# A cross-attention loop on one core: row 1, the query scales, the last row's low halves, the value products and the output products change places

## The reference

```python
x = x + xattn(layernorm(x), ctx)     # 256 tokens of 512, 4096 keys of 128
x = x + attn(layernorm(x))           # self-attention, 16 heads
x = x + ffn(layernorm(x))            # quantised, 1408 wide

def xattn(hidden_q, kv_c):
    q_hk  = (hidden_q @ Wq.T).reshape(B, S, 16, 128)
    q_big = rope(einsum('bshk,hkq->bshq', q_hk, w_kc_q))        # 384 wide
    kv_r  = rope(kv_c)
    q_r   = einsum('bshq,hqr->bhsr', q_big, W_qr)               # 64 wide
    k_r   = einsum('bld,hdr->bhlr', kv_r, W_kr)
    attn  = softmax(einsum('bhsr,bhlr->bhsl', q_r, k_r))
    ctx_c = einsum('bhsl,bld->bhsd', attn, kv_r)
    ctx   = einsum('bhsd,hkd->bhsk', ctx_c, w_kc_kv)            # the value product
    return merge_heads(ctx) @ Wo.T                              # the output product
```

## Time and profile before

| | us |
|---|---|
| median of the runs (3) | 564.32 |
| lowest and highest | 563.91, 564.53 |
| the profiled execution, its span | 564.2 |

### The profile page before, as it was taken

The page is one execution under the profiler, slowest core; times in us unless marked ns, Lnnn a source line. Parts: engine busy times, 40 slices in busy tenths (PEclk is TensorE's granted clock), DMA queues, the critical chain, the costliest instruction groups (busy, mean ns, idle before and its releaser), DMA issues.

```text
span 564.2 us, 10021 instructions
## 1 busy us (share of the span) xinstructions
PE 528.2 (94%) x3799; PEld 353.0 (63%) x3803; DVE 468.4 (83%) x708; ACT 366.0 (65%) x447; POOL 159.0 (28%) x202
## 2 busy tenths in 40 slices
PE   7899976799999999999999999999997998999996
PEld 3767643366666666666667666766676784455443
DVE  3566997999989999999999999999996447478686
ACT  2125433888788688688688787787786444886441
POOL 2378965101202202202202202202000001496501
PEclk9989999999999999999999999999998998999999
DMA  8979468399999999999999999999999997500001
GB/s 314 345 259 288 156 116 220 87 200 196 198 195 200 202 197 203 208 209 212 203 204 195 203 204 194 198 210 195 204 198 178 226 416 305 238 1 1 1 0 38
DMA packets 287806, 107.41 MB, mean 190 GB/s; under 512 B 276896, under 2 KB 277920, under 8 KB 286368
## 3 DMA queue, kind: packets, MB, share of 16 engines
q1 hardware_dynamic: 287776, 107.01, 87.6%
HBM read 37.26 MB, written 0.52 MB: 67 GB/s over the span
## 4 chain that ended last, share of the span: by engine, by line
PE 57%; DVE 17%; POOL 8%; DMA 6%; issue 6%; ACT 4%; SPq 0%; ACTq 0%; DVEq 0%; POOLq 0%
PE ps L665 15%; PE ps L667 8%; PE ps L647 7%; PE ps L649 7%; PE ps L648 7%; DMA pT<-split 6%; POOL qrope L498 5%; DVE rows L1273 4%; DVE split L1255 3%; PE ps L767 3%; POOL keys L509 2%; POOL stage L510 1%; PE ps L876 1%; PE ps L615 1%; PE ps L617 1%
## 5 line engine op out<-in xcount | busy, mean ns | idle before, releaser
L665 PE MATMUL ps<-pT,VH 128*128 128x256 f16 x1024 | 196.6, 274 | 2.1 <-DMA pT<-split 2.0
L667 PE MATMUL ps<-pT,VL 128*128 128x128 f16 x1024 | 183.3, 220 | 0.0
L1273 DVE TENSOR_SCALAR_CACHE_REDUCE rows<-ps,qback 128x1024 f32<-128x1024 f32 x128 | 163.5, 1280 | 16.0 <-PE ps L649 15.9
L1033 ACT ACTIVATE split<-rows,rz 128x2048 f16<-128x2048 f32 x64 | 124.7, 1994 | 67.8 <-DVE rz L1221 67.7
L1255 DVE SCALAR_TENSOR_TENSOR split<-rows,rz,split 128x2048 f16<-128x2048 f32 x64 | 150.3, 2350 | 1.3 <-issue 1.2
L1019 ACT ACTIVATE rows<-rows,negm 128x2048 f32<-128x2048 f32 x64 | 127.2, 1987 | 0.2 <-DVE negm L1278 0.2
L665 PEld LDWEIGHTS ps<-pT,VH 128*128 128x128 f16 x1024 | 100.5, 98 | 42.6 <-DMA pT<-split 4.8
L667 PEld LDWEIGHTS ps<-pT,VL 128*128 128x128 f16 x1024 | 100.6, 98 | 27.5
L528 POOL TENSOR_TENSOR ctx_c<-acc 128x128 f32<-128x128 f32 x32 | 24.7, 772 | 296.8 <-ACT acc L1008 296.8
L647 PE MATMUL ps<-KH,qcur 128*128 128x512 f16 x256 | 97.1, 379 | 3.3 <-DVE rows L1273 3.3
L649 PE MATMUL ps<-KH,qcur 128*128 128x512 f16 x256 | 97.0, 379 | 0.0
(11 more groups left out here) (175 smaller groups left out, 638.3 us busy)
## 6 DMA issues: line engine op xcount, KB each, us to landing
w_sb<-w SPq DMA_DIRECT2D x3, 2816.0 KB, 15.6
wq_sb<-wq SPq DMA_DIRECT2D x4, 1024.0 KB, 7.3
wo_sb<-wo SPq DMA_DIRECT2D x16, 256.0 KB, 4.2
wkcq_sb<-wkcq SPq DMA_DIRECT2D x4, 768.0 KB, 10.3
keys<-ctxT SPq DMA_DIRECT2D x8, 256.0 KB, 7.1
stage<-ctxT SPq DMA_DIRECT2D x16, 128.0 KB, 9.0
stage<-kcos SPq DMA_DIRECT2D x8, 256.0 KB, 9.0
stage<-ksin SPq DMA_DIRECT2D x8, 256.0 KB, 9.5
```

The costliest lines, as they stand in the source:

```text
L665: nc.tensor.matmul(bank(6 + r % 2, 0, 256), VH[:, 4 * b + k, :], p.rearrange("p x q -> p (x q)"), start=(b == 0 and k == 0), stop=False)
L667: last = nc.tensor.matmul(bank(6 + r % 2, 0, 128), VL[:, 4 * b + k, :], p[:, 0, :], start=False, stop=(b == 7 and k == 3))
L1033: nc.scalar.activation(split[:, split_slot(r, half), :, 0, :], rows[:, k, half * 2048:(half + 1) * 2048].rearrange("p (b k) -> p b k", k=1 ...
L1273: nc.vector.tensor_scalar(rows[:, k, c * 1024:(c + 1) * 1024], ps[:, score_bank(s) * 512:(score_bank(s) + 2) * 512], qback[:, r // 2:r // ...
```

## The change

- **Row 1 ahead of the last heads' queries.** TensorE issues steps 0 to 9 (row 0 and two of row 1) at `p` 18, two more at 19, four at 20, so that both rows stand before the loop. ScalarE takes row 0's two exponentials at `p` 20 ahead of the last two heads' copies, and loads the exponential's table at `p` 17 with a one-column operation.
- **The second query scale inside turn 1**: `query_part` at VectorE's step 5, `query_total` at TensorE's step 10, `query_factor` at VectorE's step 11. The wait for it moves from row 0's to row 1's first values.
- **Loads of `wo` heads 8 to 15**: one behind the transposes of each of rows 4 to 11, instead of all behind the last row.
- **Last turn**: the low halves of row 31 at VectorE's steps 4 and 5 (before: 8 and 10); value products 0 to 3 together at step 8, the others at 16, 17, 18, in banks 0, 1, 4, 5 in turn, with a wait for the fourth product before; their copies at 6 to 9 and 17 to 19; the splits of `wo` at 11 to 16, 20 and 21.
- **Output products by tile**: tile 0 to its end, then tile 1; the last value product behind head 8 of tile 0.

Cut to what is spoken of (functions of ScalarE that only move up in the file are left out):

```diff
-    SPLIT_STEPS = (12, 14, 16, 17, 18, 19, 20, 21)
+    SPLIT_STEPS = (11, 12, 13, 14, 15, 16, 20, 21)
     PRODUCT_STEPS = (18, 19, 20, 21, 22, 23)
+    VALUE_STEPS = (8, 8, 8, 8, 16, 17, 18)
+    CONTEXT_STEPS = (6, 7, 8, 9, 17, 18, 19)
+    VALUE_BANK = (0, 1, 4, 5)
...
             for r in range(2 * XH):
                 turn_row(r)
-            for h in range(XH // 2, XH):
-                sp.dma_start(wo_part(wo_sb, h), wo[:, h, :]).then_inc(wo_in[h // 4], 16)
+                if 4 <= r < 4 + XH // 2:
+                    h = XH // 2 + r - 4
+                    sp.dma_start(wo_part(wo_sb, h), wo[:, h, :]).then_inc(wo_in[h // 4], 16)
...
-                wait(pe, ctxl_lo_done, n - 1)
+                wait(pe, ctxl_lo_done, n - 3)
                 for a in range(2):
-                    last = nc.tensor.matmul(bank(n % 2, a * TOK, (a + 1) * TOK), wkv_sb[:, 2 * n + a, :],
+                    last = nc.tensor.matmul(bank(VALUE_BANK[n % 4], a * TOK, (a + 1) * TOK), wkv_sb[:, 2 * n + a, :],
...
+                if isinstance(i, int) and i == 1 and s == 10:
+                    query_total(1)
+                if last_turn(i) and s == VALUE_STEPS[0]:
+                    for n in range(VALUE_STEPS.count(s)):
+                        value_product(n)
...
+                        pe.wait_ge(qf_done, XH)
+                    if isinstance(i, int) and row == 1 and b == 0:
                         pe.wait_ge(qfac_done, 2)
-                        pe.wait_ge(qf_done, XH)
...
-                if last_turn(i) and s % 2 == 0 and 2 <= s < XH:
-                    value_product(s // 2 - 1)
+                if last_turn(i) and s > VALUE_STEPS[0] and s in VALUE_STEPS:
+                    value_product(VALUE_STEPS.index(s))
...
-                    first = TURN - 16 + (0, 4, 6, 8)[p - 18]
-                    for s in range(first, TURN - 16 + (4, 6, 8, 8)[p - 18]):
+                    first = TURN - 16 + (0, 10, 12, 16)[p - 18]
+                    for s in range(first, TURN - 16 + (10, 12, 16, 16)[p - 18]):
                         attention_step(0, s)
-            query_total(1)
-
-            attention_loop(pe, attention_step, EARLY, AVLAG)
-            for first in (0, XH // 2):
-                for t in range(TT):
-                    for h in range(len(PRODUCT_STEPS) if t == 0 and first == 0 else first, first + XH // 2):
-                        output_product(t, h)
-                        if first == 0 and t == 1 and h == 1:
-                            value_product(XH // 2 - 1)
+
+            attention_loop(pe, attention_step, 2 * EARLY, AVLAG)
+            for t in range(TT):
+                for h in range(len(PRODUCT_STEPS) if t == 0 else 0, XH):
+                    output_product(t, h)
+                    if t == 0 and h == len(PRODUCT_STEPS) + 2:
+                        value_product(XH // 2 - 1)
...
+                if last_turn(i) and s in CONTEXT_STEPS:
+                    context_high(CONTEXT_STEPS.index(s))
+                if last_turn(i) and s in SPLIT_STEPS:
+                    output_weight_high(SPLIT_STEPS.index(s))
...
+                if p == 17:
+                    nc.scalar.activation(warm[:, 1:2], ones[:, 0:1], ACT.Exp).then_inc(warm_done, 1)
...
+                if p == 20:
+                    attention_step(0, TURN - 8)
+                    attention_step(0, TURN - 7)
...
-            attention_loop(act, attention_step, 0, AVLAG)
+            attention_loop(act, attention_step, NCH + 2, AVLAG)
...
+                    if not isinstance(i, int) or row < 2 * XH - 1:
+                        row_low(row, r, s % 8 // 2)
+                if last_turn(i) and s in (4, 5):
+                    row_low(2 * XH - 1, 5, s - 4)
+                if isinstance(i, int) and i == 1 and s == 5:
+                    query_part(1)
+                if isinstance(i, int) and i == 1 and s == 11:
+                    query_factor(1)
...
-                    context_low(s // 2 - 1)
+                if last_turn(i) and s in CONTEXT_STEPS:
+                    context_low(CONTEXT_STEPS.index(s))
...
-            query_part(1)
-            query_factor(1)
```

More of the change, by code:

```diff
@@ L959, in raw_sum @@
                 nc.scalar.activation(absolute[:, :], keys[:, key], ACT.Abs, accum_out=kpart[:, n:n + 1]).then_inc(kabs_done, 1)
[L961 to L967, removed]
[L968 to L989 removed]
             def context_high(n):
                 act.wait_ge(ctxl_ps, n + 1)
[L994 removed]
+                nc.scalar.activation(ctxl_hi[:, 2 * n:2 * n + 2, :].rearrange("p h t -> p (h t)"), bank(VALUE_BANK[n % 4]), ACT.Copy)\
                     .then_inc(ctxl_hi_done, 1)
@@ new lines, in _ @@
+            for p in range(STEPS):
+                if p == 17:
+                    nc.scalar.activation(warm[:, 1:2], ones[:, 0:1], ACT.Exp).then_inc(warm_done, 1)
+                if p % 2 == 0 and p < XH:
+                    act.wait_ge(qhk_done, p // 2 + 1)
+                    nc.scalar.activation(qhk[:, p:p + 2, :].rearrange("p h t -> p (h t)"), bank(0), ACT.Copy)\
+                        .then_inc(qhk_copied, 1)
+                n = p - 6
+                if p == 20:
+                    attention_step(0, TURN - 8)
+                    attention_step(0, TURN - 7)
+                if n >= 0 and n % 2 == 0 and n < XH:
+                    act.wait_ge(qabs_done, n // 2 + 1)
+                    for a in range(2):
+                        nc.scalar.activation(QF[:, n + a, :], absorbed(a), ACT.Copy).then_inc(qf_done, 1)
+                        wait(act, qpart_done, n + a)
+                        nc.scalar.activation(qabsolute[:, :], absorbed(a), ACT.Abs, accum_out=qpart[:, n + a:n + a + 1])\
+                            .then_inc(qpart_done, 1)
+                n = p - 5
+                if n >= 0 and n % 2 == 0 and n < XH:
+                    act.wait_ge(qr_done, n + 2)
+                    wait(act, qabs_done, n // 2 - 1)
+                    nc.scalar.activation(qrT[:, n // 2 % 2, :], bank(6, 0, TOK), ACT.Copy).then_inc(qr_copied, 1)
+                for n in range(1, NCH):
+                    if RAW_STEP[n] == p:
+                        raw_sum(n)
+                for n in range(NCH):
+                    if HIGH_STEP[n] == p:
+                        key_high(n)
+                if p == 15:
+                    act.wait_ge(qhk_done, XH // 2)
+                    act.wait_ge(qfac_done, 1)
+                    nc.scalar.activation(qcur[:, 2, 0], QF[:, 0, :], ACT.Identity, scale=qfac[:, 0:1]).then_inc(qcur_first, 1)
@@ L1233, in key_scale, with row_low @@
                 dve.wait_ge(kscale_done, 2)
+            def row_low(row, r, half):
+                k = r % 3
+                dve.wait_ge(hi_done, 2 * row + half + 1)
+                nc.vector.scalar_tensor_tensor(out=split[:, split_slot(r, half), :, 1, :],
+                                               in0=rows[:, k, half * 2048:(half + 1) * 2048].rearrange("p (b k) -> p b k", k=128),
+                                               scalar=rz[:, k:k + 1], in1=split[:, split_slot(r, half), :, 0, :],
+                                               op0=ALU.mult, op1=ALU.subtract).then_inc(lo_done, 1)
             def query_part(k):
```

35 lines of the change are left out of this document (2 added, 33 removed).

## The result

The changed kernel takes **566.86 us** (median of 19 runs, 563.91 to 569.2), the kernel before 564.32 beside it (19 runs, 560.98 to 566.95). The ratio is 1.0037, with a 95% interval of 1.002 to 1.0055: **slower by 2.1 us** by that ratio, 2.5 by the medians. Forecast were 561.9 and, as a range, 558.6 to 565.2.

What follows compares the result with a forecast made beforehand. TensorE was taken as the bound, with the transpose queue without margin until about 223 us. Loads net of ramp 1.4, last rows -2.2, tiles -0.4, clock -1.75, returned 0.6 gave -2.35: 561.9, range 558.6 to 565.2.

Steps and rivals of the forecast that it cites:

- What bounds the kernel: TensorE is busiest; before about 223 us every microsecond put into SyncE's transpose queue is paid by TensorE.
- some seven: Transpose queue, 113.2 to 238.9: 8.0 us lost in some seven long landings, 1.1 each, read as instruction loading.
- The ramp: Setup to first transpose: row 1's scores ahead of line 718 start the first low half and first transpose 2.3 us earlier.
- The moved query scale: Before row 4's first score: TensorE waits 0.7 us for qcur, so keeps 1.6 of the ramp's 2.3 us.
- The eight loads: Transpose queue, rows 4 to 11: 0.62 us a load, row 10's transpose lands 1.4 us later, last two add nothing.
- The rival of the blocked queue: Each load blocks the queue like a long landing, 1.7 us: 568 to 570, slower than before; chance 0.13.
- The last three rows: Rows 29 to 31: value product's 2.7 us wait goes, transposes pace; sixth output product 2.2 us earlier (1.6 to 2.8).
- the third rival: The end is not won: waits for transposes of rows 29 to 31 replace the removed one; 564.2, chance 0.25.
- Products by tile: Sixth output product to transposes of z: 20.1 us instead of 20.46, -0.4, with TensorE waiting 1.5 after product 8.
- The clock at the join: Join to self-attention: with only 0.64 us of standstill left, 2.4 GHz expected in the projections, -1.75 us.
- The 0.6 that I gave back later: After the join, ScalarE becomes the later engine near 490, so 0.6 us of the gain is returned.
- The sum: Whole kernel: -2.35 us, a span of 561.85 and a median time of 561.9.

Runs made afterwards that it cites:

- The changed part alone: The kernel before with only the setup and ramp part of the change (row 1's scores and second query scale moved): 561.93 us, ratio 0.9945.
- the form with the later loads: Changed kernel with one wo load behind every second row from row 12 to 26, instead of behind each of rows 4 to 11: 563.32 us, ratio 0.9982.
- The old last turn: Changed kernel with the wo loads behind the last transpose and the last turn as before, products still by tile: 562.49 us, second run 564.06 us.

## Why the prediction was wrong

**What bounds the kernel: right.** The warning that every microsecond put into the queue before 223 us is paid by TensorE is what happened; I put too few microseconds behind it. One reading was loose: the four long landings on the chain start at 124.0, 140.1, 200.8 and 216.8, two pairs 16 us apart and not one even row. The whole queue has seven landings of 6 us and more in rows 0 to 10, which is the "some seven" of the working.

**The ramp: right.** First exponential 96.82 (forecast 96.5), first low half 104.08 (103.85), first transpose 106.46 (106.2). Counted from the first score, which this part does not move, the first transpose comes after 18.59 us, for 20.39 and 21.52 in the two profiles of before. The changed part alone is worth 3.1 us (ratio 0.9945, so 1.8 to 4.5).

**The moved query scale: right where the ramp ran at full clock, wrong in the changed kernel.** I let TensorE keep 1.6 us at row 4's first score, behind a wait of 0.7 for `qcur`. Row 4's first score in the kernel before, in the changed kernel and in the form with the later loads:

```profile
124.25 0.38 PE L647 MATMUL ps<-KH,qcur 128*128 128x512 f16 x1
...
124.00 0.38 PE L656 MATMUL ps<-KH,qcur 128*128 128x512 f16 x1
...
121.48 0.39 PE L656 MATMUL ps<-KH,qcur 128*128 128x512 f16 x1 [0.50 <-POOL qcur L526]
```

The changed kernel kept 0.25 (the 1.0 above is at row 4's first value matmul, 32 us later) and did not wait for `qcur`: the low clock from 108.8 to 115.6 lay ahead of it and had made TensorE late already. From the first score matmul it is 36.1 us in both. In the form with the later loads, whose ramp ran at full clock, it is 34.5, 1.6 less, with the wait of 0.5. A clock that falls behind a wait which the change itself lengthens (1.29 us before, 2.35 now) was missing from this step. The sum went by the transposes and took nothing from it.

**The eight loads: the step that failed.** At 0.62 us each I had row 10's second quarter 1.4 us later; it was 4.2. The bounds, 0.49 from the issue and 0.755 from a stretch full of loads, were both taken where none of these transposes ran. Among the transposes a load cost 0.92 to 1.06 in the queue, and 1.05 worked back from TensorE's own delay: -2.07 + 6 x 1.05 = 4.2. The last two cost 0.26 more, where I had none. The rival of the blocked queue was nearest in kind; it asked for 1.2 a load, and 1.05 together with the failure of the next step was enough. The Trainium skill, *DMA: Bandwidth & Descriptors*, Issuing engines are not separate DMA queues, says that all issuers share 16 engines; here SyncE issues the loads and the transposes alike, so no run tests that sentence. The 0.60 estimated from the 435 GB/s of the table in the Trainium skill, *DMA: Bandwidth & Descriptors*, is too low for this place, and the measured 1.05 decides.

**The last three rows: the second step that failed.** I forecast -2.2; it was -0.2 and -0.3 in the two profiles of the changed kernel. The waits for transposes came as the third rival has them, 5.0 us in place of 2.7 and 0.9, though none was over 1.7 and no low clock came with them. My own count had the order of events right and lost 2.1 us in three places (times less the 4.49 by which row 28 was late): row 31's first quarter was used at 437.7 instead of 436.8, its second landed after 6.37 us and held TensorE for 0.68, and the work behind came to 12.7 instead of 12.2. The old last turn at full clock takes 41.83 us in its one such profile, so by the windows only its low clock was to be won: 0.6 us where it lasted 3.4, as in both profiles of before. The run times leave room for more, as said above.

**Products by tile: right.** 20.20 us from the sixth product to the transposes of `z` (forecast 20.1, before 20.46), with a wait of 1.3 for `wo_lo` (forecast 1.5).

**The clock at the join: right.** Timeline of TensorE, the first 16 projection matmuls:

```profile
477.06 3.67 PE L775 MATMUL ps<-wink_sb,hTn 128*128 128x512 f32 x8 [0.64 <-ACT hTn L1067]
480.57 3.60 PE L775 MATMUL ps<-winq_sb,hTn 128*128 128x512 f32 x8
```

They take 7.11 us where they took 8.80: -1.69, forecast -1.75. The 0.6 that I gave back later was not lost: from the projections to the end are 89.44 us, before 91.09, a gain of 1.65.

**The sum**: forecast 1.4 - 2.2 - 0.4 - 1.75 + 0.6 = -2.35. The trace: 4.23 + 0.26 - 0.21 - 0.33 - 1.65 = +2.30. Of the 4.65 between them 2.8 are the loads' price, 2.0 the last rows; the rest cancels. The range failed because it took only one of the two as uncertain: its upper end stopped at the third rival, with the loads at 0.62.

## What to carry over

Before a transfer is moved into a queue that runs in step with the bottleneck, read the margin (use less landing) along the whole queue, and price the transfer there, not in a stretch of its own kind; here the same eight loads cost 6.4 us in rows 4 to 11, 2.4 in the last rows when spread over rows 12 to 26, and little or nothing behind the last transpose or in the setup. When a wait is removed, ask what the engine's work would wait for with that wait at zero: here the transposes were as late as the value product, and by the windows only the clock that had fallen behind the wait could be won. Judge a stretch by more than one profile where a low clock comes in some of them, and look for the same state in the other forms before a form gets the credit for it.

## What was not expected of the hardware

- A plain 256 KB load among back-to-back transposes cost 0.92 to 1.06 us of the queue, against 0.755 in a stretch full of loads; a 128 KB one 0.64.
- Behind the same wait the granted clock fell in some runs and not in others, and for different times: behind the 2.7 us wait of the value product 3.4 us (four profiles), 6.9 (one), none (one); behind the 2.35 us wait in the ramp 6.8 (seven), 3.4 (three), none (three).
- The spread of one kernel's times went with its mean granted clock in some sessions. Of 21 runs of the kernel before in one session two at a mean clock of 1.000 took 561.66 and 561.75 us, nine at 0.991 took 562.6 to 566.3, one at 0.982 took 568.61. The 19 runs of the changed kernel do not show it: three at 1.000 took 565.37 to 566.01, six at 0.997 took 566.44 to 569.2. The time to the first score, which differs by up to 1.9 us between two profiles of one kernel, is another part of the spread.
- Landings of 6 us and more for the transposes are in every profile in rows 0 to 10, five to eight of them, and in none from row 11 to row 28, wherever the loads stood. The traces also record transfers of instructions, and the two go together: in the 17 profiles every one of the 151 landings of 6 us and more (those of the last rows included) has such a transfer starting between its issue and its landing, and of the 2025 others 261 have one. In the kernel before, eleven lie between 108 and 240 us and none between 280 and 405. That the one causes the other was not tested by an experiment.
